# Moving the quantisation of the second FFN weight out of the attention stage, and broadcasting a row of scales by DMA

## The chip, the cores and the metric

The kernel runs on the 8 cores of one Trainium2 chip. Each core works on its own two sequences of 2048 tokens (16 sequences in all), and no data goes between cores. The metric is the device time of the slowest core, in microseconds, as the median over runs. The profile is one execution on its slowest core, core 6.

## The reference, cut to what matters

```python
# attention half, per sequence (S=2048, D=1024)
q, k, v = split(x @ w_qkv.T)
att = softmax(q @ k.T / 32)
y = einsum('bqk,bvd->bqd', att, v) @ w_fc.T + b_fc   # k and v are summed apart
x = LN(x + (LN(x + y) * gamma + beta))
# FFN half (H=4096): bit_linear, depthwise conv of 3 taps over tokens, SiLU, bit_linear
act_quant(t)    = clip(round(t * s), -128, 127) / s,  s = 127 / max|t| over the row
weight_quant(w) = clip(round(w * s), -1, 1) / s,      s = 1 / mean|w|
h = silu(conv(act_quant(x) @ weight_quant(w1).T))
x = LN(x + act_quant(h) @ weight_quant(w2).T)
```

In the einsum the rows of the attention matrix are summed by themselves, so the attention half needs each softmax row only as its own sum; the scores are computed all the same.

## The kernel before, in words

The program is a series of blocks. In a block each engine has its own list of instructions, executed in order; between blocks all engines meet. `p.wait(engine, sem, n)` puts a wait for a semaphore into an engine's list, and everything behind it on that engine waits too. SP (sync), ACT (scalar) and POOL (gpsimd) also issue DMAs, in the order of their lists.

1. **P0, W0.** Constants are loaded; w1T and w2T are streamed through SBUF to get the mean absolute values, in two buffers: the load of chunk c is issued when the buffer of chunk c-2 has been read (L214 to L231). `wqcols` then holds the scales of both weights.
2. **For each of two sequences:** `APRO` (q and k from x, the column sums of v), then `A3`. `A3` goes over 16 tiles of 128 queries: 32 matmuls of scores into four PSUM banks (L646), maxima on DVE (L655), exponentials with sums on ACT (L664), the epilogue of the *previous* tile (layer norms and the int8 quantisation of x, L297 to L399), then the row sums (L677 to L684). At the start of the first `A3`, POOL is given the 16 loads of x and wqT that the next sequence needs (L487, L417).
3. **In each of these 32 query tiles** one chunk of w2 (128 x 1024) is quantised by `emit_w2q_chunk`: POOL loads it into `q2st` two chunks ahead (L448, L477), ACT scales it into `q2z` (L456), DVE makes the ternary values in `t2st` (L464, L467), POOL stores them to the DRAM tensor `t2q` (L472).
4. **W1** (`quantize_weights(w1T, ...)`): DVE quantises w1 straight into the SBUF tensor `tw`, three instructions per chunk (L743, L746, L749), loads in two buffers.
5. **F1**, over 16 tiles of 256 tokens: 32 groups of 8 matmuls (L937), evicted by DVE with a scale (L948), conv by ACT (L961) and DVE (L825, L832), SiLU on ACT (L840). At the end of the tile DVE takes the maximum over all 4096 hidden values of each token (L977), and from it the scale of each token is worked out. The scales stand as a row in `rowbuf` (L1015); a matmul with `esel` spreads the row to 128 partitions (L1019), DVE copies it from PSUM (L1023) and doubles it three times (L1028), so that `s2bc8` holds 8 copies of the row in each partition. The hidden values are then quantised in four groups (`emit_quant_A`: L852 and L863; `emit_quant_B`: L875 to L888), inside the loop of the *next* tile; the first group's L852 stands ahead of the next tile's first eviction in DVE's list. After the loop of a tile SP issues the store of the quantised tile before it (L898) and eight transposing loads and one small load for the tile after next (L811, L815).
6. **F2**: SP loads `t2q` back into `tw` in 32 pieces (L1067), waits for them, loads three tiles of hidden values (`load_hq`, L1084) and TensorE multiplies (L1113, L1122); the FFN epilogue follows tile by tile.

Of the kernel before, what the change touches and what calls it, by code (L numbers as in the profile page):

```python
# [81 lines left out]
def build_program(cfg: Cfg, debug=False):  # L82
# [35 lines left out]
    t2q = nc.dram_tensor("t2q", [HC * 128, D], BF16, kind=ik).ap()  # L118
# [26 lines left out]
    zcol = sb("zcol", (128, 1), F32)  # L145
# [58 lines left out]
    p.op("vector", lambda v: v.memset(zcol[:], 0.0))  # L204
# [231 lines left out]
    q2st = attn_stack.enter_context(nc.sbuf_tensor("q2st", [128, 2 * D], F32))  # L436
    q2z = attn_stack.enter_context(nc.sbuf_tensor("q2z", [128, D], F32))
    t2st = attn_stack.enter_context(nc.sbuf_tensor("t2st", [128, D], BF16))
    w2_ld, w2_z, w2_st, w2_sz = {}, {}, {}, {}
    w2_next = [0]  # L440

    def emit_w2q_chunk(p, c):
        par = c % 2
        lsems = (dW, gX)
        ssems = (gg, gW)
        if c == 0:
            for cc in range(min(2, HC)):
                p.op("gpsimd", lambda g, cc=cc: g.dma_start(  # L448
                    out=q2st[:, (cc % 2) * D:(cc % 2 + 1) * D],
                    in_=w2T[cc * 128:(cc + 1) * 128, :]),  # L450
                    inc=lsems[cc % 2], k=16)
                w2_ld[cc] = lsems[cc % 2].n
        p.wait("scalar", lsems[par], w2_ld[c])
        if c >= 1:
            p.wait("scalar", vv, w2_z[c - 1])
        p.op("scalar", lambda sc, par=par: sc.activation(  # L456
            out=q2z[:], in_=q2st[:, par * D:(par + 1) * D],
            func=AF.Identity, scale=wqcols[:, 1:2], bias=zcol[:, 0:1]),
            inc=ssm)
        w2_sz[c] = ssm.n  # L460
        p.wait("vector", ssm, w2_sz[c])
        if c >= 1:
            p.wait("vector", ssems[(c - 1) % 2], w2_st[c - 1])
        p.op("vector", lambda v: v.tensor_scalar(  # L464
            out=t2st[:], in0=q2z[:], scalar1=0.5, scalar2=None,
            op0=ALU.is_ge))
        p.op("vector", lambda v: v.scalar_tensor_tensor(  # L467
            out=t2st[:], in0=q2z[:], scalar=-0.5, in1=t2st[:],
            op0=ALU.is_le, op1=ALU.subtract), inc=vv)
        w2_z[c] = vv.n  # L470
        p.wait("gpsimd", vv, w2_z[c])
        p.op("gpsimd", lambda g, c=c: g.dma_start(  # L472
            out=t2q[c * 128:(c + 1) * 128, :],
            in_=t2st[:]), inc=ssems[par], k=16)
        w2_st[c] = ssems[par].n
        if c + 2 < HC:
            p.op("gpsimd", lambda g, cc=c + 2: g.dma_start(  # L477
                out=q2st[:, (cc % 2) * D:(cc % 2 + 1) * D],
                in_=w2T[cc * 128:(cc + 1) * 128, :]),
                inc=lsems[par], k=16)  # L480
            w2_ld[c + 2] = lsems[par].n
    import math
    W2K = max(1, math.ceil(HC / (NSEQ * NGRP * NQT)))
# [9 lines left out]
    for s_i in range(NSEQ):  # L493
# [129 lines left out]
        if True:  # L623
            if True:
# [72 lines left out]
                if s_i == NSEQ - 1:
                    while w2_next[0] < HC:
                        emit_w2q_chunk(p, w2_next[0])
                        w2_next[0] += 1  # L700
# [60 lines left out]
    with nc.sbuf_tensor("xqF", [128, 2 * DC * WW], BF16) as xqF, \  # L761
# [18 lines left out]
        p.wait("sync", dW, dW.n)  # L780
        p.wait("sync", gX, gX.n)
        p.wait("sync", gg, gg.n)
        p.wait("sync", gW, gW.n)
# [124 lines left out]
        for i in range(NT1):  # L908
# [340 lines left out]
```

How the kernel before makes its waits and increments, by code:

```python
        def cl(e, fn=fn, tgt=tgt, drain=drain):  # L52
            ins = fn(e)
            if tgt is not None:
                ins.then_inc(*tgt)
            if drain:
                e.drain()
# [3 lines left out]
    def wait(self, eng, sem, val):  # L61
        self.items[eng].append(lambda e, h=sem.h, v=val: e.wait_ge(h, v))
```

## Time and profile before

| | before |
|---|---|
| median of 3 runs | 4906.04 us (4904.6 to 4906.8) |
| time of the profiled execution | 4904.37 us |
| its span on core 6, from first to last instruction | 4902.7 us |
| spans of the eight cores | 4890.1 to 4902.7 us |
| mean granted TensorE clock | 0.701 to 0.704 of full speed |
| busy: DVE, PE, ACT, POOL | 66%, 37%, 21%, 1% |
| share of the chain that ended last: DVE, PE, issue, ACT | 38%, 12%, 4%, 3% |

The busy share says how long an engine had an instruction in work. The chain is the work that ended last, followed back through what released each step. A line such as `[0.51 <-ACT q2z L456]` in a timeline says that the engine had idled 0.51 us before this instruction and that ACT's instruction of line 456 ended that. In what follows, stages are read with timelines, since an average over the span mixes stages with different limits.

### The profile page before, as it was taken

How to read it: one execution, taken by the hardware profiler on the slowest of the kernel's cores; microseconds unless marked ns; L12 is line 12 of the kernel's file. 1: busy time of each engine (PE TensorE's matmuls, PEld its weight loads, DVE VectorE, ACT ScalarE, POOL GpSimd, SP SyncE). 2: the span in 40 equal slices, each digit the busy share in tenths (PEclk: the TensorE clock that was granted, in tenths of full speed). 3: DMA queues.
4: the chain of work that ended last, by engine and by line, in shares of the span. 5: the costliest groups of instructions: out<-in, count | busy, mean ns of one | idle time of the engine just before them, and what ended most of it. 6: DMA issues, size and time to landing. Idle time of an engine off the chain costs nothing.

```text
span 4902.7 us, 35148 instructions; the slowest of 8 cores (4890.1 to 4902.7 us)
## 1 busy us (share of the span) xinstructions
PE 1817.2 (37%) x8417; PEld 920.3 (19%) x8500; DVE 3256.1 (66%) x4491; ACT 1007.3 (21%) x1805; POOL 60.2 (1%) x116
## 2 busy tenths in 40 slices
PE   0046232217532311323333323333333332307999
PEld 0022011103111101211221112111121221203444
DVE  3313087872278777788888888888888888872333
ACT  2200022210022221222222222222222222210111
POOL 0000000000000000000000000000000000000000
PEclk9998666658766655665656666666566666658999
DMA  5521422221222214000000000000000000016543
GB/s 167 151 39 35 99 73 71 69 67 18 69 67 69 71 54 147 7 23 23 3 21 24 23 23 2 22 23 24 23 3 21 23 23 18 4 35 197 167 142 108
DMA packets 196433, 275.74 MB, mean 56 GB/s; under 512 B 64514, under 2 KB 132354, under 8 KB 194180
## 3 DMA queue, kind: packets, MB, share of 16 engines
q1 hardware_dynamic: 163716, 189.57, 13.2%
q0 software_dynamic: 14080, 41.95, 3.7%
q10 hardware_dynamic: 18432, 41.97, 2.2%
q14 instruction: 135, 1.11, 0.1%
q8 instruction: 70, 1.15, 0.1%
HBM read 196.86 MB, written 83.91 MB: 57 GB/s over the span
## 4 chain that ended last, share of the span: by engine, by line
DVE 38%; PE 12%; issue 4%; ACT 3%; DVEq 2%; DMA 1%; SPq 1%; ACTq 0%
DVE accb L885 6%; DVE maxM L977 5%; DVE vt L832 4%; DVE vt L825 4%; DVE rbuf L882 4%; DVE ubuf L948 3%; DVE hqst L888 3%; DVE dsb L875 3%; PE ps_d L1122 2%; DVE zscr L852 2%; PE ps_s L1122 2%; PE ps_c L1113 2%; PE ps_s L1113 2%; DVEq L57 2%; ACT vt L961 1%
## 5 line engine op out<-in xcount | busy, mean ns | idle before, releaser
L937 PE MATMUL ps_a<-xqF,tw 128*128 128x258 bf16 (+1 forms) x1024 | 216.2, 382 | 1002.4 <-DVE ubuf L948 775.7
L646 PE MATMUL ps_s<-kf,qf 128*128 128x512 bf16 x1002 | 289.2, 455 | 641.9 <-ACT disc L664 636.8
L961 ACT ACTIVATE vt<-ubuf,cbcol,cwcol 128x256 f32<-128x256 f32 x512 | 307.7, 601 | 921.7 <-DVE ubuf L948 891.9
L937 PE MATMUL ps_s<-xqF,tw 128*128 128x258 bf16 (+1 forms) x2048 | 316.7, 309 | 52.2 <-DVE ubuf L948 49.5
L885 DVE TENSOR_TENSOR accb<-accb,rbuf 128x2048 bf16<-128x2048 bf16 x256 | 313.4, 1224 | 19.7 <-issue 0.9
L937 PEld LDWEIGHTS ps_a<-xqF,tw 128*128 128x128 bf16 x1024 | 123.5, 128 | 1078.9 <-issue 1038.0
L825 DVE SCALAR_TENSOR_TENSOR vt<-ubuf,cwcol,vt 128x256 f32<-128x256 f32 x512 | 248.1, 485 | 84.1 <-issue 57.2
L832 DVE SCALAR_TENSOR_TENSOR vt<-ubuf,cwcol,vt 128x256 f32<-128x256 f32 x512 | 248.1, 485 | 39.2 <-issue 1.1
L840 ACT ACTIVATE ubuf<-vt 128x256 f32<-128x256 f32 x512 | 213.7, 417 | 269.3 <-DVE vt L832 251.8
L646 PEld LDWEIGHTS ps_s<-kf,qf 128*128 128x128 bf16 x1024 | 113.1, 113 | 818.7 <-issue 743.5
L984 PE MATMUL ps_c<-identf,maxM 128*128 128x128 f32 x64 | 19.1, 454 | 643.6 <-DVE maxM L977 643.6
L977 DVE TENSOR_REDUCE maxM<-ubuf 128x256 f32<-128x8192 f32 x16 | 247.5, 15466 | 10.2 <-ACT ubuf L840 10.2
L863 ACT ACTIVATE iqq<-zscr,c 128x2048 int32<-128x2048 f32 x64 | 128.1, 2002 | 603.6 <-DVE zscr L852 603.6
L1122 PE MATMUL ps_d<-tw,hq 128*128 128x512 bf16 x512 | 195.6, 382 | 126.1 <-DMA hq<-hqs 125.1
L937 PEld LDWEIGHTS ps_s<-xqF,tw 128*128 128x128 bf16 x2048 | 210.5, 109 | 163.8 <-issue 116.0
L937 PE MATMUL ps_b<-xqF,tw 128*128 128x258 bf16 (+1 forms) x1024 | 217.5, 384 | 12.4 <-DVE ubuf L948 10.8
L507 PE MATMUL ps_a<-xfb,wbuf 128*128 128x512 bf16 x501 | 126.3, 394 | 225.1 <-DMA wbuf<-wqT 82.0
L1122 PE MATMUL ps_s<-tw,hq 128*128 128x512 bf16 x512 | 194.0, 379 | 1.1
L882 DVE TENSOR_SCALAR rbuf<-dsb 128x2048 bf16<-128x2048 bf16 x256 | 177.6, 694 | 20.0 <-issue 0.4
L1113 PE MATMUL ps_c<-tw,hq 128*128 128x512 bf16 x492 | 188.0, 382 | 0.0
L1113 PE MATMUL ps_s<-tw,hq 128*128 128x512 bf16 x491 | 186.1, 379 | 0.0
L875 DVE SCALAR_TENSOR_TENSOR dsb<-zscr,iqq 128x2048 bf16<-128x2048 f32 x64 | 146.7, 2292 | 21.4 <-issue 10.8
(144 smaller groups left out, 3026.8 us busy)
## 6 DMA issues: line engine op xcount, KB each, us to landing
hqs<-hqst SPq DMA_DIRECT2D x16, 2048.0 KB, 8.9
wstage<-w1T SPq DMA_DIRECT2D x8, 2048.0 KB, 8.7
wstage<-w2T SPq DMA_DIRECT2D x32, 512.0 KB, 4.4
xres<-x_tm SPq DMA_DIRECT2D x32, 512.0 KB, 4.7
q2st<-w2T POOLq DMA_DIRECT2D x32, 512.0 KB, 3.8
x1s<-x1t ACTq DMA_DIRECT2D x32, 512.0 KB, 5.2
qstage<-w1T SPq DMA_DIRECT2D x8, 2048.0 KB, 8.4
xres<-x1s SPq DMA_DIRECT2D x32, 512.0 KB, 7.4
```

The costliest lines, as they stand in the source:

```text
L646: t.matmul(ps_s[kb][:, 0:KBW], qf[:, dc * S + qcol: dc * S + qcol + 128], kf[:, dc * S + kb * KBW: dc * S + (kb + 1) * KBW], start=(dc == ...
L825: v.scalar_tensor_tensor(out=vt2[:, cpar * T1W2:cpar * T1W2 + T1], in0=ubuf[:, hc * T1W2:hc * T1W2 + T1], scalar=cwcol[:, 3 * hc:3 * hc + ...
L832: v.scalar_tensor_tensor(out=vt1[:, cq * T1W2:cq * T1W2 + T1], in0=ubuf[:, hc * T1W2 + 2:hc * T1W2 + 2 + T1], scalar=cwcol[:, 3 * hc + 2:3 ...
L840: p.op("scalar", lambda sc, hc=hc, cq=cq: sc.activation(out=ubuf[:, hc * T1W2 + 1:hc * T1W2 + 1 + T1], in_=vt1[:, cq * T1W2:cq * T1W2 + T1 ...
L875: p.op("vector", lambda v, FD=FD: v.scalar_tensor_tensor(out=dsb[:, 0:FD], in0=zscr[:, 0:FD], scalar=128.0, in1=iqq[:, 0:FD], op0=ALU.add, ...
L882: p.op("vector", lambda v, FD=FD, thr=thr: v.tensor_scalar(out=rbuf[:, 0:FD], in0=dsb[:, 0:FD], scalar1=thr, scalar2=None, op0=ALU.is_ge))
L885: p.op("vector", lambda v, FD=FD: v.tensor_tensor(out=accb[:, 0:FD], in0=accb[:, 0:FD], in1=rbuf[:, 0:FD], op=ALU.add))
L937: lo=lo, hi=hi, w0=w0, W=W: t.matmul(bank[:, 0:W], tw[:, dc * H + hc * 128: dc * H + hc * 128 + 128], xqF[:, (par * DC + dc) * WW + (lo - w0):
L961: p.op("scalar", lambda sc, hc=hc: sc.activation(out=vt1[:, (hc % 4) * T1W2:(hc % 4) * T1W2 + T1], in_=ubuf[:, hc * T1W2 + 1:hc * T1W2 + 1 ...
L977: p.op("vector", lambda v: v.reduce_max(out=maxM[:, 0:T1], in_=_ap(ubuf, 1, [[HC * T1W2, 128], [1, T1], [T1W2, HC]]), axis=AX.X, apply_abs ...
L1113: banks=banks: t.matmul(banks[0][:, 0:DH], hq2[:, slot + hc * T1 + sq * 128: slot + hc * T1 + sq * 128 + 128], tw[:, hc * D + 0:hc * D + D ...
L1122: banks=banks: t.matmul(banks[1][:, 0:DH], hq2[:, slot + hc * T1 + sq * 128: slot + hc * T1 + sq * 128 + 128], tw[:, hc * D + DH:hc * D + ...
```

## The change

Three edits.

- **w2 is no longer quantised in the attention stage.** `emit_w2q_chunk`, its three buffers, its semaphores, the DRAM tensor `t2q` and the reload of it at the start of F2 go. In their place `quantize_weights(w2T, HC, D, 1)` stands as a block between F1 and F2 and writes `tw` directly: 32 chunks of 128 x 1024, each with one load and three DVE instructions, in two buffers.
- **The row of scales is spread by DMA.** The matmul with `esel`, the PSUM copy and the three doubling copies go. SP stores `rowbuf` (256 fp32) to a DRAM tensor `s2row`, waits for that store, and loads `s2bc8` from it with a source that repeats the row for 128 partitions and 8 copies: 1 MB in runs of 1 KB.
- **DVE waits for that load** ahead of the first `emit_quant_A` of a tile, and no longer right behind the row's computation.

```diff
-    t2q = nc.dram_tensor("t2q", [HC * 128, D], BF16, kind=ik).ap()
+    s2row = nc.dram_tensor("s2row", [2, T1], F32, kind="Internal").ap()
...
-    def emit_w2q_chunk(p, c):
...
-                    for _ in range(W2K):
-                        if w2_next[0] < HC:
-                            emit_w2q_chunk(p, w2_next[0])
-                            w2_next[0] += 1
...
+            if g0 == 0:
+                p.wait("vector", s2sems[i % 2], s2_ld[i])
             p.op("vector", lambda v, g0=g0, ng=ng, FD=FD, s28=s28: v.tensor_tensor(
...
             p.wait("vector", mm, mm.n)
+            if i >= 1:
+                p.wait("vector", s2sems[(i - 1) % 2], s2_ld[i - 1])
             p.op("vector", lambda v: v.tensor_copy(
                 out=rowbuf[0:1, 0:T1], in_=ps_d[0:1, 0:T1]), inc=vv)
             ev_row = vv.n
-            p.wait("tensor", vv, ev_row)
-            p.op("tensor", lambda t: t.matmul(
-                ps_d[:, 0:T1], esel[:], rowbuf[:, 0:T1], start=True, stop=True),
-                inc=mm)
-            p.wait("vector", mm, mm.n)
-            p.op("vector", lambda v: v.tensor_copy(
-                out=s2bc8[:, 0:T1], in_=ps_d[:, 0:T1]), inc=vv)
-            w = T1
-            while w < NQG * T1:
-                cw2 = min(w, NQG * T1 - w)
-                p.op("vector", lambda v, w=w, cw2=cw2: v.tensor_copy(
-                    out=s2bc8[:, w:w + cw2], in_=s2bc8[:, 0:cw2]))
-                w += cw2
-            p.op("vector", lambda v: v.engine_nop(), inc=vv)
+            sem = s2sems[i % 2]
+            if i >= 2:
+                p.wait("sync", sem, s2_ld[i - 2])
+            p.wait("sync", vv, ev_row)
+            p.op("sync", lambda s, i=i: s.dma_start(
+                out=s2row[i % 2:i % 2 + 1, 0:T1], in_=rowbuf[0:1, 0:T1]),
+                inc=sem, k=16)
+            p.wait("sync", sem, sem.n)
+            if i >= 1:
+                p.wait("sync", vv, lastA_ev[i - 1])
+            p.op("sync", lambda s, i=i: s.dma_start(
+                out=_ap(s2bc8, 0, [[NQG * T1, 128], [T1, NQG], [1, T1]]),
+                in_=_ap(s2row.tensor, (i % 2) * T1,
+                        [[0, 128], [0, NQG], [1, T1]])), inc=sem, k=16)
+            s2_ld[i] = sem.n
...
+    quantize_weights(w2T, HC, D, 1)
...
-        for c in range(HC):
-            sem = dS if c % 2 == 0 else dSb
-            p.op("sync", lambda s, c=c: s.dma_start(
-                out=tw[:, c * D:(c + 1) * D],
-                in_=t2q[c * 128:(c + 1) * 128, :]), inc=sem, k=16)
-        t2_dS, t2_dSb = dS.n, dSb.n
-        p.wait("tensor", dS, t2_dS)
-        p.wait("tensor", dSb, t2_dSb)
```

## Rows read from the trace of the kernel before

**Rows 1.** Page, part 1: busy time and share of each engine.

```profile
PE 1817.2 (37%) x8417; PEld 920.3 (19%) x8500; DVE 3256.1 (66%) x4491; ACT 1007.3 (21%) x1805; POOL 60.2 (1%) x116
```

**Rows 2.** Windows, F1: stretch, its length, busy of each engine, PEclk, DMA share, GB/s.

```profile
1936.00:4399.00 2463.00, 781.55 (x4256) 491.01 (x4256) 2027.53 (x2752) 650.82 (x1089) 0.00 (x0) 0.63 0.07 18
```

**Rows 3.** Timeline, first two query tiles: start, length, engine, line, out<-in, idle before.

```profile
540.84 9.00 PE L646 MATMUL ps_s<-kf,qf 128*128 128x512 bf16 x31 [8.18 <-ACT disc L664]
541.57 0.75 DVE L684 TENSOR_SCALAR atile<-wrowbc,colsb 128x1024 f32<-128x1024 f32 x1
...
606.95 0.53 POOL L448 DMA_DIRECT2D q2st<-w2T  x1 [3.48 <-issue]
...
614.22 2.99 DVE L655 TENSOR_REDUCE colsb<-ps_s 128x1 f32<-128x512 f32 x4 [0.17 <-issue]
```

**Rows 4.** Timeline, a query tile in the steady state.

```profile
700.28 0.75 DVE L684 TENSOR_SCALAR atile<-wrowbc,colsb 128x1024 f32<-128x1024 f32 x1
...
703.70 2.99 DVE L655 TENSOR_REDUCE colsb<-ps_s 128x1 f32<-128x512 f32 x4 [0.16 <-issue]
...
710.48 9.52 PE L646 MATMUL ps_s<-kf,qf 128*128 128x512 bf16 x32 [20.75 <-ACT disc L664]
...
733.85 2.99 DVE L655 TENSOR_REDUCE colsb<-ps_s 128x1 f32<-128x512 f32 x4 [0.17 <-issue]
```

**Rows 5.** Timeline, second query tile of the second sequence.

```profile
1358.51 2.99 DVE L655 TENSOR_REDUCE colsb<-ps_s 128x1 f32<-128x512 f32 x4 [5.81 <-PE ps_s L646]
```

**Rows 6.** Timeline, the boundary between the second and the third tile of F1.

```profile
2161.76 0.58 SPq L815 DMA_DIRECT2D f1bc<-f1s  x1
...
2178.26 0.41 DVE L1015 COPY rowbuf<-ps_d 1x256 f32<-1x256 f32 x1 [1.26 <-PE ps_d L1010]
...
2183.33 2.29 DVE L852 TENSOR_TENSOR zscr<-ubuf,s2bc 128x2048 f32<-128x2048 f32 x1
2185.77 2.00 ACT L863 ACTIVATE iqq<-zscr,c 128x2048 int32<-128x2048 f32 x1 [28.92 <-DVE zscr L852]
...
2189.47 0.48 DVE L825 SCALAR_TENSOR_TENSOR vt<-ubuf,cwcol,vt 128x256 f32<-128x256 f32 x1 [0.16 <-ACT vt L961]
```

**Rows 7.** Timeline, SP: a 4 KB row stored to DRAM, and the load that waits for it.

```profile
486.28 0.30 SPq L565 DMA_DIRECT2D vrow_d<-vrow  x1
487.56 3.67 SPq L569 DMA_DIRECT2D colsb<-vrow_d  x8
```

**Rows 8.** DMA issues: out<-in, issuer, count, KB each, median us from issue to landing.

```profile
hqs<-hqst SPq DMA_DIRECT2D x16, 2048.0 KB, 8.9
...
wf<-wfcT SPq DMA_DIRECT2D x16, 512.0 KB, 4.0
...
f1bc<-f1s SPq DMA_DIRECT2D x12, 129.0 KB, 3.2
```

**Rows 9.** Windows, while three 4 KB rows are broadcast to 128 partitions: the columns as in rows 2.

```profile
5.00:12.00 7.00, 0.00 (x0) 0.00 (x0) 0.00 (x0) 0.00 (x0) 0.00 (x0) 1.00 0.84 215
```

**Rows 10.** Timeline, from the end of F1 to the first matmul of F2.

```profile
4396.72 2.29 DVE L888 TENSOR_TENSOR hqst<-accb,iqq 128x2048 bf16<-128x2048 bf16 x1
...
4408.45 19.40 SPq L1067 DMA_DIRECT2D tw<-t2q  x32
4437.06 13.81 SPq L1084 DMA_DIRECT2D hq<-hqs  x3
4447.44 0.10 PEld L1113 LDWEIGHTS ps_c<-tw,hq 128*128 128x128 bf16 x1 [125.43 <-issue]
```

**Rows 11.** Timeline, W0 on w2T: two of its steps on ACT, nine apart.

```profile
123.87 1.06 ACT L227 ACTIVATE wabs<-wstage 128x1024 f32<-128x1024 f32 x1 [1.50 <-DMA wstage<-w2T]
...
149.19 1.06 ACT L227 ACTIVATE wabs<-wstage 128x1024 f32<-128x1024 f32 x1 [1.93 <-DMA wstage<-w2T]
```

**Rows 12.** Groups of instructions by form: count, busy us, mean ns, idle before.

```profile
L467 DVE SCALAR_TENSOR_TENSOR t2st<-q2z,t2st 128x1024 bf16<-128x1024 f32 x32 | 39.2, 1224 | 2.4
...
L464 DVE TENSOR_SCALAR t2st<-q2z 128x1024 bf16<-128x1024 f32 x32 | 22.2, 693 | 87.0 <-ACT q2z L456 86.7 <-issue 0.2
```

More of the change, by code:

```diff
@@ L144, in build_program @@
     c128 = sb("c128", (128, 1), F32)
-    zcol = sb("zcol", (128, 1), F32)
     gammaBC = sb("gammaBC", (128, D), F32)
@@ L175, in build_program @@
     gg = Sem(E(nc.semaphore("gg")))
-    dW = Sem(E(nc.semaphore("dW")))
-    gW = Sem(E(nc.semaphore("gW")))
-    gX = Sem(E(nc.semaphore("gX")))
     p = PB(nc, "P0")
@@ L203, in build_program @@
     p.op("vector", lambda v: v.memset(rowbuf[:], 0.0))
-    p.op("vector", lambda v: v.memset(zcol[:], 0.0))
     p.op("vector", lambda v: v.memset(wsmat[:], 0.0))
@@ L435, in build_program @@
     dGq = {}
[L436 to L440, printed above, removed]
-    def emit_w2q_chunk(p, c):
[L443 to L483, printed above, removed]
     def emit_A0(p, s_i):
@@ L692, in build_program @@
                     epi_q[qt] = (row0, par, sto, dep, ldsem)
-                    for _ in range(W2K):
-                        if w2_next[0] < HC:
-                            emit_w2q_chunk(p, w2_next[0])
-                            w2_next[0] += 1
[L697 to L700, printed above, removed]
                 qt_last = NGRP * NQT - 1
@@ L779, in build_program @@
         p.wait("sync", dS, dS.n)
[L780 to L783, printed above, removed]
         def tgeom(i):
@@ L801, in build_program @@
         ld_cnt = {}
+        s2_ld = {}
+        lastA_ev = {}
+        s2sems = (dS, dSb)
         def emit_loads(i):
@@ L857, in emit_quant_A @@
             ev_z = vv.n
+            lastA_ev[i] = ev_z
             p.wait("scalar", vv, ev_z)
@@ L1059, in build_program @@
         p.wait("sync", dXb, dXb.n)
-        p.wait("sync", dG, dG.n)
-        p.wait("sync", dW, dW.n)
-        p.wait("sync", gX, gX.n)
-        p.wait("sync", gg, gg.n)
-        p.wait("sync", gW, gW.n)
-        for c in range(HC):
-            sem = dS if c % 2 == 0 else dSb
-            p.op("sync", lambda s, c=c: s.dma_start(
-                out=tw[:, c * D:(c + 1) * D],
-                in_=t2q[c * 128:(c + 1) * 128, :]), inc=sem, k=16)
-        t2_dS, t2_dSb = dS.n, dSb.n
-        p.wait("tensor", dS, t2_dS)
-        p.wait("tensor", dSb, t2_dSb)
         hq_ld = {}
@@ L1149, in build_program @@
     p.wait("gpsimd", dG, dG.n)
-    p.wait("gpsimd", dW, dW.n)
-    p.wait("gpsimd", gX, gX.n)
-    p.wait("gpsimd", gg, gg.n)
-    p.wait("gpsimd", gW, gW.n)
     p.run()
```

## The prediction, made before the changed kernel ran

> **What bounds the kernel now.** I read the page first: DVE is busy for two thirds of the span, TensorE for little more than a third [rows 1]. Then I cut the span into stages. In F1, half of the whole time, DVE is busy 2027.5 of 2463 us and ACT and PE far less [rows 2]: DVE's list sets the pace, and what stands between its instructions at a tile's boundary is paid 16 times. The timelines of the attention stage say the same with two exceptions. In the steady state DVE begins the maxima L655 of the next tile with no wait for TensorE, and the 9.52 us of matmuls end at 720.0, far ahead of their use at 733.85 [rows 4]. The exceptions are the first chunk of each sequence: in the first, DVE has finished L684 at 542.32 and begins L655 at 614.22, because the first w2 load is behind POOL's 16 loads for the next sequence and issued at 606.95 [rows 3]; in the second, L655 waits for TensorE anyway [rows 5]. At the end of F1 everything waits for DMAs for 48.4 us, from L888's end at 4399.01 to the first matmul's weights at 4447.44 [rows 10]. All three edits touch such places, so I price them by timeline.
>
> **Part 1: w2 leaves the attention stage (a gain).** In the steady state the stretch from L684's end (701.03) to L655 (703.70) is 2.67 us: a wait for ACT, 0.69 and 1.22 us of work [rows 4, 12]. Without the chunk, a semaphore wait of 0.16 us is left, so 2.51 us are saved. This holds for 30 chunks: all but the first of each sequence. 30 x 2.51 = 75.3 us. Chunk 16, the first of the second sequence, saves nothing, for L655 waits for TensorE [rows 5]. Chunk 0 saves its stall: its matmuls end at 540.84 + 9.00 = 549.84 [rows 3], so L655 can begin at 549.95 in place of 614.22, a gain of 64.3 us. Together -139.6 us. What is next late there? Not TensorE: the period falls from 30.15 (733.85 - 703.70) to 27.6 us, and the matmuls end some 16.3 us after L655 begins (710.48 + 9.52 - 703.70) [rows 4]. POOL's 16 loads now run beside a busy DVE; all were issued by 606.95, some 80 us into the stage [rows 3], and the second sequence needs them only when 16 tiles of 27.6 us, 442 us, are over, so even at three times the length they are hidden; without that cover each further us would count fully.
>
> The page "SBUF — State Buffer" of the Trainium skill states in its note on the "DVE blocks DMA" trap that descriptors made by GpSimd wait while DVE runs certain fp32 instructions. By it these loads would be slower in the new kernel; no stretch of rows here shows 16 of them beside a busy DVE, and by the bound above it would change the sum only past some 440 us of loading.
>
> **Part 2: the row of scales goes by DMA (a loss).** Now: L1015 ends at 2178.67, L852 begins at 2183.33, 4.66 us later [rows 6]. After: SP issues the store about 0.08 us behind L1015, is free to do so (its last issue for the tile ended at 2162.3 [rows 6]), and can issue the load 1.28 us later, as for the 4 KB row in [rows 7]. The load of 1 MB takes D, then DVE wakes in 0.1. So L852 begins 1.46 + D behind L1015. The memset and the scaling of the next tile's factors are done in this time, so TensorE starts the next tile earlier, and the four evictions behind L852 no longer wait for it: L825 came 6.14 us after L852's start [rows 6]; ACT needs L852's 2.29, 0.15, its own 2.00, 0.14 and 0.60 of the first conv instruction, 5.3 with the wait, so 0.84 us come back in 15 of 16 tiles. Queued behind DVE's wait are these evictions, and ACT and TensorE wait with them; on SP nothing is queued that is due for over 100 us. Sum: 16 x (1.46 + D - 4.66) - 15 x 0.84 = 16 D - 63.8.
>
> D has no row. Loads of 512 KB land in 4.0 us, 2 MB in 8.9 us also in runs of 512 bytes [rows 8]; on the line between them 1 MB takes 5.6, of which 2.4 are fixed. But the source is one 1 KB row read 1024 times. Broadcasts of 4 KB rows moved at 215 GB/s on average with other small transfers between them [rows 9]: 1.05 MB / 215 = 4.9 us, with the fixed 2.4 that is 7.3, and somewhat less without those others. Broadcasting one 1 KB row to 128 partitions takes 3.2 us for 129 KB [rows 8]; with the 1.28 of [rows 7] as its fixed part, eight times the rest is 15.4, so 16.6 in all is the upper bound. The lower bound is the 4.0 of half the bytes. I take 6.0, between the first two and nearer to the size rows, since the 215 GB/s were shared: 16 x 6.0 - 63.8 = +32 us. The bounds give 0 and +202.
>
> The page "DMA: Bandwidth & Descriptors" of the Trainium skill (Anatomy of one DMA) states 2.0 us for any DMA and 436 GB/s on top, for the other way of issuing. By it the store and the load together are an estimated 6.4 us where I take 7.3, and the sum of this part would be an estimated +18.
>
> **Part 3: w2 between F1 and F2 (a loss).** Three instructions per chunk: 0.75 (L684 has this shape), 0.69 and 1.22 us [rows 4, 12], 2.83 with gaps, 3.0 with a wait. Load c is issued when chunk c-2 is finished. So two chunks take one load and one computation, if the load is the longer. W0 has the same scheme on the same tensor: nine steps in 25.32 us, 2.81 each, and 2 x 2.81 - 1.06 = 4.56 us from release to use [rows 11]. The 4.0 us load of the same size [rows 8] gives 4.1. W1 asks for less per us, so I take 4.2: (4.2 + 2.83) / 2 = 3.5 us per chunk; the bounds are 3.0 (DVE alone) and 3.7. The first load is behind the 2 MB store of the last tile: issued right behind L888's end at 4399.0, landed 8.9 later [rows 8, 10], then 512 KB more (1.6 us by the line of part 2), so the first chunk begins at about 4410. 4410 + 31 x 3.5 + 2.8 = 4521.3 is its end. A change of block costs 0.5 (the store lands at 4408.0, L1067 follows at 4408.45), and from `load_hq`'s issue to the first matmul it is 4447.44 - 4437.06 = 10.4 [rows 10]. TensorE starts at 4532.2 in place of 4447.4: +85 us; with the bounds +69 and +91. Nothing hides it, since F2 needs all of `tw` and all engines meet between blocks. The reload's 32 issues and their wait are in the 48.4 us that are replaced. F2 itself is unchanged.
>
> **The sum.** -139.6 + 32 + 85 = -23 us. The profiled execution took 4904.4, so 4882; the median of the runs is 1.7 above that execution: **4883 us**.
>
> **The rivals.**
>
> *The broadcast is slow.* 1024 reads of one 1 KB row of DRAM may not run at the rate of a spread load. For it speaks the 129 KB broadcast at 3.2 us, hardly faster than four times its size [rows 8]; against it, 215 GB/s with 4 KB rows [rows 9]. With D at the 8.9 of a 2 MB transfer the part costs +79 us and the kernel takes 4930; at the upper bound 5053. It decides for slower (by over 0.2%) from D = 8.0 on, where 16 D - 63.8 - 54.6 = 9.8. Chance 0.18.
>
> *The edits cancel.* D between 6.8 and 8.0 puts the sum within 0.2% (9.8 us, about what a measurement can tell from no change); 7.4 gives 4905. For it: the 7.3 of the broadcast row. Chance 0.14.
>
> *The losses are smaller.* D near 4.5, and chunks at DVE's 3.0 us, since fewer bytes per us are asked than in W0: -139.6 + 8 + 69 = -62, so 4843. Chance 0.08.
>
> *The stall only moves.* If the first tile's epilogue then waits for its residual load, or the second sequence for POOL's loads, part 1's 64 us are lost: 4947. Against it: POOL's loads have 360 us of cover, and SP issues the residual loads with nothing ahead of them. Chance 0.03.
>
> The likeliest case has what is left, 0.57. **Numbers.** Faster 0.57 + 0.08 = 0.65, same 0.14, slower 0.21. The range runs from 4846 (the smaller losses nearly in full) to 4936 (D at 8.9 with chunks at 3.7), leaving out the slowest broadcasts and the moved stall; the likeliest case alone reaches from 4862 to 4895.
>
> **What would show it.** L655 of the second query tile begins at about 550 and the period is 27.6 us. At each boundary of F1, L852 begins 7.5 us after L1015's end, released by the DMA into `s2bc8`, and L825 5.3 after L852. W1's second use shows DVE idle some 0.7 us before each L743, ended by a DMA, and 111 us in all. I am wrong if the broadcast's landing is far from 6.0, where each us is worth 16; if the chunks are off 3.5, each 0.1 worth 3; or if something in F1 that this trace does not show changes its pace.

## The result: slower, by the broadcast alone

| | before | after |
|---|---|---|
| median (10 runs of each) | 4907.42 us (4902.93 to 4970.47) | 5137.61 us (5086.43 to 5229.99) |
| ratio | | 1.0438 [1.0391, 1.0484] |
| time of the profiled execution | 4904.37 us | 5086.43 us |
| its span on the slowest core | 4902.7 us (core 6) | 5084.9 us (core 4) |

The forecast was 4883 us with 4846 to 4936 as its range. The ratios leave out the runs in which one die's cores were granted a lower clock and took longer; the medians and ranges take in all. The runs of the changed kernel lie further apart than those of the kernel before, and its profiled execution, the one that everything below is worked out from, is the fastest of the ten, 51 us under the median; no trace shows where those 51 us lie. Since core 4 is its slowest core, I compare with core 4 of before, whose span was 4896.3 us: 188.6 us are to be found.

The page of after, part 1 (busy time of each engine), and of part 5 the group of the quantisation's first step (count, busy us, mean ns, then the idle time ahead of it):

```profile
PE 1827.8 (36%) x8468; PEld 925.7 (18%) x8468; DVE 3251.0 (64%) x4458; ACT 967.7 (19%) x1773; POOL 25.7 (1%) x52
...
L792 DVE TENSOR_TENSOR zscr<-ubuf,s2bc 128x2048 f32<-128x2048 f32 x64 | 146.7, 2292 | 336.0 <-DMA s2bc<-s2row 331.2
```

DVE has as much to do as before [rows 1]. What is new is idle time: 331.2 us ahead of the 16 first L792 (L852 of before), 20.7 us each, and a DMA ends it. I then cut the span at the marks at which the prediction cut it. First the attention stage, which ends where F1's first load is issued (the list of one tile's instructions: count, min/median/max ns, first and last start), after:

```profile
L749 SPq DMA_TRANSPOSE xqF<-xqs x128: 1111/1245/6854, 1776.3 to 4060.9; - x128
```

The same of before, core 4:

```profile
L811 SPq DMA_TRANSPOSE xqF<-xqs x128: 1113/1244/6837, 1917.8 to 3990.3; - x128
```

F1 begins 141.5 us earlier. Timeline of after's first query tiles on core 4, which answers to [rows 3, 4]:

```profile
532.43 8.82 PE L593 MATMUL ps_s<-kf,qf 128*128 128x512 bf16 x32 [8.19 <-ACT disc L611]
533.16 0.75 DVE L631 TENSOR_SCALAR atile<-wrowbc,colsb 128x1024 f32<-128x1024 f32 x1
...
541.36 2.99 DVE L602 TENSOR_REDUCE colsb<-ps_s 128x1 f32<-128x512 f32 x4 [7.45 <-PE ps_s L593]
...
568.13 0.75 DVE L631 TENSOR_SCALAR atile<-wrowbc,colsb 128x1024 f32<-128x1024 f32 x1
569.04 2.99 DVE L602 TENSOR_REDUCE colsb<-ps_s 128x1 f32<-128x512 f32 x4 [0.16 <-issue]
...
579.58 0.53 POOL L412 DMA_DIRECT2D wbuf<-wqT  x1 [18.22 <-issue]
...
596.72 2.99 DVE L602 TENSOR_REDUCE colsb<-ps_s 128x1 f32<-128x512 f32 x4 [0.52 <-issue]
```

The second tile's maxima L602 no longer wait for a w2 chunk: they follow their matmuls, which end at 541.25. From L631's end (568.88) to L602 (569.04) are the forecast 0.16 us, and the period is 27.68 us (596.72 - 569.04). On core 6, the core of [rows 3], the second tile's L602 begins at 549.81, where "about 550" was forecast.

Now a boundary in F1, the first, to hold against [rows 6]:

```profile
1880.27 0.41 DVE L958 COPY rowbuf<-ps_d 1x256 f32<-1x256 f32 x1 [1.26 <-PE ps_d L951]
1880.76 0.24 SPq L965 DMA_DIRECT2D s2row<-rowbuf  x1
...
1881.94 0.40 SPq L971 DMA_DIRECT2D s2bc<-s2row  x1
...
1905.35 2.29 DVE L792 TENSOR_TENSOR zscr<-ubuf,s2bc 128x2048 f32<-128x2048 f32 x1 [23.72 <-DMA s2bc<-s2row]
1907.74 2.00 ACT L804 ACTIVATE iqq<-zscr,c 128x2048 int32<-128x2048 f32 x1 [48.88 <-DVE zscr L792]
1910.58 0.48 DVE L763 SCALAR_TENSOR_TENSOR vt<-ubuf,cwcol,vt 128x256 f32<-128x256 f32 x1 [0.59 <-ACT vt L902]
```

And the last one:

```profile
4412.97 0.36 SPq L971 DMA_DIRECT2D s2bc<-s2row  x1
4429.78 2.29 DVE L792 TENSOR_TENSOR zscr<-ubuf,s2bc 128x2048 f32<-128x2048 f32 x1 [18.12 <-DMA s2bc<-s2row]
```

From the load's issue to its use, which I call D from here on (the profile gives no landing for this transfer), are 23.4 us at the first boundary and 16.8 at the last. Over the 16 boundaries of core 4 the sum is 324.6 us, 20.3 each; the means of the eight cores go from 17.7 to 20.3. From the first load to the end of the last tile F1 took 4503.43 - 1776.3 = 2727.1 us, against 4394.79 - 1917.8 = 2477.0 on core 4 of before: +250.1.

Last, from the end of F1 to F2, for [rows 10]:

```profile
4501.14 2.29 DVE L829 TENSOR_TENSOR hqst<-accb,iqq 128x2048 bf16<-128x2048 bf16 x1
4503.55 0.36 SPq L839 DMA_DIRECT2D hqs<-hqst  x1
4504.43 107.23 SPq L678 DMA_DIRECT2D qstage<-w2T  x32
4515.18 0.75 DVE L682 TENSOR_SCALAR qz<-qstage,wqcols 128x1024 f32<-128x1024 f32 x1 [11.76 <-DMA qstage<-w2T]
...
4615.38 0.75 DVE L682 TENSOR_SCALAR qz<-qstage,wqcols 128x1024 f32<-128x1024 f32 x1 [0.89 <-DMA qstage<-w2T]
4619.00 13.77 SPq L1015 DMA_DIRECT2D hq<-hqs  x3
4629.40 0.58 PE L1044 MATMUL ps_c<-tw,hq 128*128 128x512 bf16 x1 [218.34 <-DMA hq<-hqs]
```

The same two ends on core 4 of before:

```profile
4392.50 2.29 DVE L888 TENSOR_TENSOR hqst<-accb,iqq 128x2048 bf16<-128x2048 bf16 x1
...
4442.29 0.10 PEld L1113 LDWEIGHTS ps_c<-tw,hq 128*128 128x128 bf16 x1 [124.51 <-issue]
```

L829's end at 4503.43 to L1044 at 4629.40 are 126.0 us; L888's end to L1113 were 47.5: +78.5. The three stretches give -141.5 + 250.1 + 78.5 = +187.1 of the 188.6 us. The 1.5 us left are F2's. Two of the three terms are close to the forecast ones; the surprise is the wait for `s2bc8`.

### The profile page after: what moved, and what is told of

Its sections match the earlier page's. It is cut to its first block and busy times, and to the rows that moved or that the text cites. A ratio compares the mean times of both kernels' runs of the same rounds, so it can differ in the third digit from the quotient of the medians.

```text
span 5084.9 us, 34871 instructions; the slowest of 8 cores (5027.7 to 5084.9 us)
## 1 busy us (share of the span) xinstructions
PE 1827.8 (36%) x8468; PEld 925.7 (18%) x8468; DVE 3251.0 (64%) x4458; ACT 967.7 (19%) x1773; POOL 25.7 (1%) x52
## 3 DMA queue, kind: packets, MB, share of 16 engines
q1 hardware_dynamic: 180388, 214.75, 16.6%
## 5 line engine op out<-in xcount | busy, mean ns | idle before, releaser
L878 PE MATMUL ps_a<-xqF,tw 128*128 128x258 bf16 (+1 forms) x1024 | 226.8, 396 | 1237.7 <-DVE ubuf L889 1033.6
L792 DVE TENSOR_TENSOR zscr<-ubuf,s2bc 128x2048 f32<-128x2048 f32 x64 | 146.7, 2292 | 336.0 <-DMA s2bc<-s2row 331.2
L878 PE MATMUL ps_s<-xqF,tw 128*128 128x258 bf16 (+1 forms) x2048 | 327.0, 317 | 45.0 <-DVE ubuf L889 42.1
L763 DVE SCALAR_TENSOR_TENSOR vt<-ubuf,cwcol,vt 128x256 f32<-128x256 f32 x512 | 248.2, 485 | 90.1 <-issue 54.1
L1044 PE MATMUL ps_c<-tw,hq 128*128 128x512 bf16 x512 | 195.8, 382 | 218.3 <-DMA hq<-hqs 218.3
L878 PE MATMUL ps_b<-xqF,tw 128*128 128x258 bf16 (+1 forms) x1024 | 230.5, 402 | 15.3 <-DVE ubuf L889 14.0
L1044 PE MATMUL ps_s<-tw,hq 128*128 128x512 bf16 x512 | 194.0, 379 | 0.0
L823 DVE TENSOR_SCALAR rbuf<-dsb 128x2048 bf16<-128x2048 bf16 x256 | 177.6, 694 | 20.7 <-issue 1.3
```

What stands on the lines that cost most here:

```text
L763: v.scalar_tensor_tensor(out=vt2[:, cpar * T1W2:cpar * T1W2 + T1], in0=ubuf[:, hc * T1W2:hc * T1W2 + T1], scalar=cwcol[:, 3 * hc:3 * hc + ...
L823: p.op("vector", lambda v, FD=FD, thr=thr: v.tensor_scalar(out=rbuf[:, 0:FD], in0=dsb[:, 0:FD], scalar1=thr, scalar2=None, op0=ALU.is_ge))
L878: lo=lo, hi=hi, w0=w0, W=W: t.matmul(bank[:, 0:W], tw[:, dc * H + hc * 128: dc * H + hc * 128 + 128], xqF[:, (par * DC + dc) * WW + (lo - w0):
L1044: banks=banks: t.matmul(banks[0][:, 0:DH], hq2[:, slot + hc * T1 + sq * 128: slot + hc * T1 + sq * 128 + 128], tw[:, hc * D + 0:hc * D + D ...
```

## The experiments

### One part alone: which of them costs

The first kernel is the changed one with the matmul and the doubling copies put back, so it has parts 1 and 3. The second is the kernel before with the DMA broadcast alone, part 2.

```diff
 # matmul back, against the changed kernel; DMA only is the reverse on the kernel before
-            if g0 == 0:
-                p.wait("vector", s2sems[i % 2], s2_ld[i])
...
-            p.op("sync", lambda s, i=i: s.dma_start(
-                out=_ap(s2bc8, 0, [[NQG * T1, 128], [T1, NQG], [1, T1]]),
-                in_=_ap(s2row.tensor, (i % 2) * T1,
-                        [[0, 128], [0, NQG], [1, T1]])), inc=sem, k=16)
+            p.op("tensor", lambda t: t.matmul(
+                ps_d[:, 0:T1], esel[:], rowbuf[:, 0:T1], start=True, stop=True),
+                inc=mm)
```

Matmul back:

> The changed kernel with the old spreading of the scales (matmul, PSUM copy, doubling copies) put back, so only the moves of w2 are left. Theory: the broadcast by DMA is the whole loss, the moves of w2 give what the trace of the changed kernel shows, -141 us in the attention stage and +78 us between F1 and F2, so 4907 - 63 = 4844 us, a clear gain. Rival: the moves of w2 cost something in F1 too (TensorE or DVE at another pace), then F1 is longer than the 2463 us of before and the time is 4907 or above.

DMA only:

> The kernel before with only the broadcast by DMA put in; w2 stays in the attention stage. Theory: the two parts add up, so this costs what is left of the change's 230 us once the 63 us of gain are taken out: 4907 + 293 = 5200 us, between 5150 and 5240, with about 20 us from the load's issue to its use. Rival: the broadcast is slow only because the cores reach it at other times or in another order in the changed kernel; then it is clearly faster here, below 5100.

Matmul back: 4855.28 us (median of 5 runs) beside 4915.58 of before on the same chip, ratio 0.9835 [0.9693, 0.9978]. DMA only: 5206.3 us (4 runs), ratio 1.0541 [1.0413, 1.0668], with a mean D of 21.3 us over all cores. Its page has the wait in the kernel that keeps the w2 work where it was:

```profile
L858 DVE TENSOR_TENSOR zscr<-ubuf,s2bc 128x2048 f32<-128x2048 f32 x64 | 146.7, 2292 | 389.7 <-DMA s2bc<-s2row 385.2
```

So parts 1 and 3 together are a gain of 60 us between the medians, where 54.6 were forecast; the ratio's interval leaves its size open between 0.2% and 3.1%. The stages say more: with the matmul back F1 took 2475.6 us in the mean of the cores, 2476.4 before, so the rival that the moved w2 work costs something in F1 is out. With the broadcast alone F1 took 2742.6 us. The broadcast is the whole loss, also without parts 1 and 3.

### What makes the broadcast slow

Candidates: the megabyte itself, its runs of 1 KB or SBUF's side of it; or the source, one row of 1 KB read 1024 times. The first kernel reads 1024 different runs of 1 KB from `w1T`, with everything else equal; what it loads are then not the scales, so it leaves the spreading of the scales out. The second stores the row eight times side by side and reads runs of 8 KB.

```diff
 # other source: the load reads w1T
-                in_=_ap(s2row.tensor, (i % 2) * T1,
-                        [[0, 128], [0, NQG], [1, T1]])), inc=sem, k=16)
+                in_=_ap(w1T.tensor, 0,
+                        [[H, 128], [2 * T1, NQG], [1, T1]])), inc=sem, k=16)
 # 8 KB row: the store
+                out=_ap(s2row.tensor, (i % 2) * 8 * T1,
+                        [[8 * T1, 1], [T1, 8], [1, T1]]),
+                in_=_ap(rowbuf, 0, [[512, 1], [0, 8], [1, T1]])),
 # 8 KB row: the load
+                out=_ap(s2bc8, 0, [[NQG * T1, 128], [1, NQG * T1]]),
+                in_=_ap(s2row.tensor, (i % 2) * 8 * T1,
+                        [[0, 128], [1, NQG * T1]])), inc=sem, k=16)
```

Other source:

> The changed kernel with one edit: the 1 MB load reads 1024 different 1 KB runs (of w1T) in place of one row 1024 times, so size, runs and target are the same; the row is still stored and waited for. The scales in s2bc8 are then not the right ones, so the output is not the reference's. Theory (a repeated source is slow): about 5.6 us from issue to use, 16 x 15 us less than the changed kernel, so 4860 to 4880 us. Rival (1 MB in 1024 runs of 1 KB into 8 KB per partition is slow from any source): 15 to 23 us as in the changed kernel, 5080 to 5150 us.

8 KB row:

> The changed kernel with the row stored 8 times side by side (8 KB) and read by each partition as one run of 8 KB. Same bytes moved, 128 reads in place of 1024, over a source eight times as long. Theory that the length of the source region sets the rate: about 5 to 8 us, near 4880 us. Theory that it is any rereading of few bytes by all cores, whatever the region: 15 us and more, above 5050 us.

The timeline of the other source at a boundary:

```profile
2059.69 0.57 SPq L971 DMA_DIRECT2D s2bc<-w1T  x1
...
2065.65 2.29 DVE L792 TENSOR_TENSOR zscr<-ubuf,s2bc 128x2048 f32<-128x2048 f32 x1 [6.32 <-DMA s2bc<-w1T]
```

The same of the 8 KB row:

```profile
2041.94 0.33 SPq L973 DMA_DIRECT2D s2bc<-s2row  x1
...
2046.78 2.29 DVE L792 TENSOR_TENSOR zscr<-ubuf,s2bc 128x2048 f32<-128x2048 f32 x1 [6.07 <-DMA s2bc<-s2row]
```

With the other source D is 5.96 us here and 6.1 in the mean of all cores, the 6.0 of the forecast, and the kernel took 4880.69 us (one run) where the forecast said 4883. So size, run length, destination, queue and the semaphores' way are cleared: the term was right for a source that is spread. (That the time comes so near has luck in it: F1 was 8 us and the w2 block 10 us shorter there than forecast, and its slowest core, 0, came to F1's first load at 1801.2, 25 us later than core 4 of the changed kernel.) The 8 KB row has a mean D of 4.95 us and took 4860.65 us in the profiled execution and 4960.46 in the other (before: 4915.58); of so scattered a pair only the stages of the profile can be used, and D says that a row may well be repeated, if it is long.

The rate can be read from windows of the load (columns as in [rows 2], the last is GB/s). After, during its first broadcast:

```profile
1894.00:1896.00 2.00, 0.00 (x0) 0.00 (x0) 0.00 (x0) 0.00 (x0) 0.00 (x0) 0.50 0.52 36
1896.00:1898.00 2.00, 0.00 (x0) 0.00 (x0) 0.00 (x0) 0.00 (x0) 0.00 (x0) 0.50 0.60 39
1898.00:1900.00 2.00, 0.00 (x0) 0.00 (x0) 0.00 (x0) 0.00 (x0) 0.00 (x0) 0.50 0.83 79
...
1902.00:1904.00 2.00, 0.00 (x0) 0.00 (x0) 0.00 (x0) 0.00 (x0) 0.00 (x0) 0.50 1.00 87
```

The other source:

```profile
1910.00:1911.00 1.00, 1.00 (x6) 0.73 (x5) 0.00 (x0) 0.00 (x0) 0.00 (x0) 0.50 1.05 348
```

The 8 KB row:

```profile
1892.00:1893.00 1.00, 1.00 (x6) 0.69 (x5) 0.00 (x0) 0.00 (x0) 0.00 (x0) 0.50 0.98 410
```

The DMA engines are up to fully busy in each, but move 36 to 87 GB/s from the one row in these windows, against 348 and 410. A busy share of 1.00 says that packets are in work, not that bytes flow.

### How much source is enough, and does its place matter

Four more kernels, whose lines differ only in store and load: a row of 2 KB (the row twice); eight copies 1280 bytes apart, read in runs of 1 KB; eight copies 64 KB apart; and one copy per partition (128 KB) that DVE doubles three times.

```diff
 # 2 KB row (the load writes its copies in runs of 2 KB too)
...
+                in_=_ap(s2row.tensor, (i % 2) * 2 * T1,
+                        [[0, 128], [0, NQG // 2], [1, 2 * T1]])), inc=sem, k=16)
 # eight rows, 1280 bytes apart
+                in_=_ap(s2row.tensor, (i % 2) * 2560,
+                        [[0, 128], [320, NQG], [1, T1]])), inc=sem, k=16)
 # eight rows, 64 KB apart
+                in_=_ap(s2row.tensor, (i % 2) * 131072,
+                        [[0, 128], [16384, NQG], [1, T1]])), inc=sem, k=16)
 # 128 KB load
+                out=_ap(s2bc8, 0, [[NQG * T1, 128], [1, T1]]),
+                in_=_ap(s2row.tensor, (i % 2) * T1,
+                        [[0, 128], [1, T1]])), inc=sem, k=16)
```

2 KB row:

> The changed kernel with the row stored twice side by side (2 KB) and read by each partition in four runs of 2 KB: the dose between one row of 1 KB (about 20 us) and one of 8 KB (5.0 us). If the rate grows with the source's length, 1 MB takes half as long as from 1 KB, 2 us fixed plus 9: about 11 us. If there is a step somewhere above 2 KB, it stays near 20.

Eight rows, 1280 bytes apart:

> The changed kernel with the row stored 8 times at a distance of 1280 bytes, and the 8 copies of each partition read each from its own row. Still 1024 reads of 1 KB, still few bytes in all, but each row is read 128 times and the rows span 10 KB. Theory (what is short is the rate at which one 1 KB row of DRAM can be read by all 16 DMA engines and all cores at once): as with the 8 KB row, 5 to 7 us from issue to use. Rival (the 8 KB runs made the load fast, not the longer source): 15 us and more.

Eight rows, 64 KB apart:

> The same with the 8 rows 64 KB apart. Theory of the row as the unit: again 5 to 7 us. If the distance matters in the other direction (rows at a large power of two fall on the same part of DRAM), then as slow as one row, 15 us and more.

128 KB load:

> The changed kernel with a load of only one copy per partition (128 reads of the 1 KB row, 128 KB) and the seven other copies made by DVE as before (256, 512 and 1024 columns, 1.8 us). Theory: the slow rate hits an eighth of the bytes, so about 3.2 to 4.5 us of load and with the doubling 5 to 6.5 us from the load's issue to the quantisation; 4860 to 4885 us. If the first read of the row were what is slow, it would stay above 10 us.

Each is one run, with one run of 4909.91 us of the kernel before beside it. D is the mean over all cores and boundaries; the changed kernel and the two kernels above stand in the table too. In the kernel before, F1 took 2476.4 us.

| source of the load | D, us | least and most, us | F1, us (mean of the cores) | kernel, us |
|---|---|---|---|---|
| one row of 1 KB, 1 MB (after) | 18.8 | 14.3 to 23.6 | 2702.9 | 5086.43 (profiled) |
| eight rows 64 KB apart, 1 MB | 17.8 | 13.0 to 21.6 | 2701.7 | 5082.63 |
| one row of 2 KB, 1 MB | 9.6 | 8.0 to 16.3 | 2564.7 | 4954.16 |
| eight rows 1280 bytes apart, 1 MB | 6.2 | 5.5 to 9.1 | 2515.0 | 4918.86 |
| 1024 runs of `w1T`, 1 MB | 6.1 | 5.8 to 7.1 | 2500.1 | 4880.69 |
| one row of 8 KB, 1 MB | 5.0 | 4.3 to 7.8 | 2494.8 | 4860.65 (profiled) |
| one row of 1 KB, 128 KB | 3.1 | 2.9 to 4.4 | 2477.0 | 4835.66 |

The eight rows 64 KB apart, timeline:

```profile
2061.38 0.37 SPq L973 DMA_DIRECT2D s2bc<-s2row  x1
2082.59 2.29 DVE L792 TENSOR_TENSOR zscr<-ubuf,s2bc 128x2048 f32<-128x2048 f32 x1 [22.43 <-DMA s2bc<-s2row]
```

The eight rows 1280 bytes apart, page, part 5:

```profile
L792 DVE TENSOR_TENSOR zscr<-ubuf,s2bc 128x2048 f32<-128x2048 f32 x64 | 146.7, 2292 | 132.1 <-DMA s2bc<-s2row 127.2
```

The 128 KB load, timeline:

```profile
2035.13 0.33 SPq L974 DMA_DIRECT2D s2bc<-s2row  x1
...
2038.09 1.56 DVE L793 COPY s2bc<-s2bc 128x256 f32<-128x256 f32 x3 [3.30 <-DMA s2bc<-s2row]
2039.72 2.29 DVE L795 TENSOR_TENSOR zscr<-ubuf,s2bc 128x2048 f32<-128x2048 f32 x1
```

The 2 KB row, windows on core 0 during its first load:

```profile
1878.00:1880.00 2.00, 2.00 (x12) 1.36 (x10) 0.00 (x0) 0.00 (x0) 0.00 (x0) 0.50 0.59 175
1880.00:1882.00 2.00, 2.00 (x11) 1.41 (x10) 0.00 (x0) 0.00 (x0) 0.00 (x0) 0.50 0.71 143
```

Twice the row halves D, and its best window, 175 GB/s, is twice the 87 of the 1 KB row: here the rate went with the length of the row. Eight rows close together, still read in runs of 1 KB, are as good as a spread source. Eight rows 64 KB apart are as bad as one. So it is not the number of different rows that counts, but where in DRAM they lie: whatever serves the repeated reads is shared by addresses 64 KB apart and not by those 1280 bytes apart.

What that is, these runs don't say, nor whether it is the distance of 64 KB or its being a power of two that counts: no rows at a padded distance of that size were run. The theory of the row as the unit, expected for these rows, failed.

Of the 128 KB load 2.96 us go by from issue to use at this boundary: at 80 GB/s 1.6 of them are an estimate for the bytes. With this load and DVE's copies F1 is as long as with the matmul, and the kernel took 24 us less than the least expected.

F1's times follow from D and one more thing. The stores of eight copies hold the load back: it is issued 2.09 us behind such a store and 1.25 behind a store of one copy (means over all cores), which is 13 us in 16 tiles. So the 8 KB row should be 16 x (4.95 - 6.10) + 13 = 5 us faster in F1 than the other source, and is 5.3; the rows 1280 bytes apart 15 us slower, and are 14.9.

The kernel times follow less well. The one with rows 1280 bytes apart took 4918.86 us, the other source 4880.69, and 15 of these 38 us are F1's. Its core 6, with the longest span (4917.3), waits 7.95 us at a boundary (127.2 / 16), core 0 7.4, with a span of 4862.3. Core 6 came into F1 16 us later than core 0 (first load at 1784.8 and 1768.5), took 8 us longer over it and 31 over what follows, where its granted clock was 0.93 in F2 and that of core 0 1.00. So 47 of the 55 us between the two cores lie outside the stage in question, and I take nothing from that kernel's time.

### The gain without the loss

Four kernels test parts 1 and 3 by other means. The first is the kernel before with POOL's 16 loads dealt out over the query tiles, one each, so that the first w2 chunk is not behind them. The second takes, on top, the doubling copies out, and L852 reads its second operand with a step of 0 over the eight groups; so the copies' 1.4 us per boundary go with no DMA in their place. The third is the changed kernel with the matmul and the same step of 0. The fourth is the third with ACT doing the first of the three steps per w2 chunk, and the first three `hq` loads issued in that block.

```diff
 # loads dealt out (kernel before)
-                if s_i + 1 < NSEQ:
-                    emit_A0(p, s_i + 1)
...
+                    if s_i + 1 < NSEQ:
+                        emit_A0_part(p, s_i + 1, qt)
 # step of 0
-            s28 = s2bc8[:, 0:FD]
+            s28 = _ap(s2bc8, 0, [[NQG * T1, 128], [0, ng], [1, T1]])
...
-            w = T1
-            while w < NQG * T1:
...
 # ACT in the w2 block
+            p.op("scalar", lambda sc, stage=stage, z=z: sc.activation(
+                out=z[:], in_=stage[:], func=AF.Identity,
+                scale=wqcols[:, 1:2], bias=zcol[:, 0:1]), inc=ssm)
```

Loads dealt out:

> The kernel before with one edit: POOL's 16 loads for the second sequence are issued one per query tile, behind that tile's w2 chunk, in place of all 16 at the start. Theory: the stall of the first chunk (72 us, of which 64 count) came from its load standing behind these 16 on POOL, so it goes and nothing else changes: 64 us less, 4843 us where before is at 4907. Rival: the stall is only moved to a later chunk or to the start of the second sequence: within 10 us of before.

Loads dealt out, step of 0:

> The same, and the three doubling copies of the scales are left out: L852 reads its second operand 8 times over from one copy of 256 columns. Theory: the instruction takes its 2.29 us as before, and at each of 16 boundaries 1.9 us of copies go, some of which TensorE's first groups need; 20 to 30 us less than the spread alone, 4813 to 4823. Rival: reading an operand again with a step of zero is slower on DVE, then 64 instructions grow and the time is above the spread alone.

Changed kernel, matmul, step of 0:

> The changed kernel with the scales spread by the matmul and read with the step of zero. Theory: the moves of w2 are worth the same as the spread of POOL's loads (-141 + 78 against -64), so within 10 us of the kernel before this one, 4810 to 4825.

The same with ACT:

> As the last, and the w2 stage between F1 and F2 is made shorter: ACT scales a chunk and so frees its buffer for the next load, DVE has two instructions per chunk in place of three, and the first three loads of hidden values are issued at the end of this stage. A chunk took 3.2 us; with the buffer freed after ACT's 1.24 us two chunks take one load and one ACT instruction, about 2.5 us each, so 23 us less, and 5 to 10 us of the first load of F2 are hidden: 4780 to 4795. Rival: the loads of all cores at this rate take longer (W0 needed 2.8 us per chunk), then 4800 or more.

| | median, us (4 runs each) | least and most | ratio to before (4909.29) |
|---|---|---|---|
| loads dealt out | 4853.8 | 4842.19 to 4870.76 | 0.9885 [0.9841, 0.9928] |
| and step of 0 | 4815.72 | 4810.71 to 4912.66 | 0.9797 [0.974, 0.9853] |
| changed, matmul, step of 0 | 4818.24 | 4817.47 to 4853.84 | 0.9827 [0.9776, 0.9879] |
| the same with ACT | 4840.4 | 4795.68 to 4853.44 | 0.9839 [0.9773, 0.9904] |

Timeline of the loads dealt out, beginning of the stage:

```profile
527.56 0.53 POOL L448 DMA_DIRECT2D q2st<-w2T  x1 [146.32 <-POOLq L65]
...
546.87 0.69 DVE L464 TENSOR_SCALAR t2st<-q2z 128x1024 bf16<-128x1024 f32 x1 [0.16 <-ACT q2z L456]
```

The first w2 load is issued at 527.56 in place of 606.95 [rows 3], DVE quantises its chunk at 546.87, and the kernel gains 55.5 us between the medians; F1's first load comes at 1852.9 in the mean of the cores, against 1916.6 before, the expected 64 us. So of part 1's gain the 64 us of the stall need no move of the w2 work at all: they were the order of POOL's list. Groups of instructions of the kernel with the step of 0:

```profile
L863 DVE TENSOR_TENSOR zscr<-ubuf,s2bc 128x2048 f32<-128x2048 f32 x64 | 146.7, 2292 | 6.0 <-issue 0.2
```

L863 (L852 of before) still takes 2292 ns, and DVE waits 6.0 us in all ahead of it. The eight copies were never needed, neither by matmul nor by DMA. Taking them out is worth 38 us between the medians, but the two intervals overlap. The traces settle the size: F1 took 2445.4 to 2448.8 us on the eight cores with the step of 0, and 2474.8 to 2476.8 on those of the kernel with the loads dealt out alone, 29 us in the means. That is the copies' own 16 x 1.4 = 23 and what stood between them and their neighbours. The other 9 us of the medians are not F1's.

By its median this is the fastest kernel of the study, faster than the kernel before and the changed one. It and the third kernel (4818.24) came out as expected (4813 to 4823, 4810 to 4825). The third kernel's interval overlaps with it, so moving the w2 work is neither shown better nor worse than dealing out the loads.

The fourth missed its expected 4780 to 4795 and is not shown faster than the third: its lowest run is the lowest of all, its median is 22 us higher. Its own edit did work: from the end of F1 to the first matmul of F2 are 107.5 us in the mean of the cores, against 126.3 in the third, with a chunk every 2.6 to 2.8 us where it took 3.2. What hides these 19 us in its profiled execution lies ahead of F1, in what both kernels share: its slowest cores, 6 and 7, come to F1's first load at 1837 and 1832, its cores 0 to 3 at 1775 to 1791.

## Why the prediction was wrong, by its steps

**What bounds the kernel, right.** DVE's list set the pace of F1, and the boundary was paid 16 times; that is why 14.3 us more per transfer became 16 x 14.3 = 229.

**Part 1, right.** -141.5 us where -139.6 were forecast. Taken apart, in the medians over the cores: the first two L655 of the first sequence were 80.2 us apart and are 17.1, a gain of 63.1 (64.3 forecast), and a query tile with a chunk took 29.98 us and takes 27.44, a gain of 2.54 (2.51 forecast). That the whole agrees within 2 us is partly luck, since the cores of after come to F1's first load over a range of 20 us (1764.5 to 1784.7). POOL's loads do get slower beside the busy DVE: on core 4 their 16 issues go over 123.6 us, 75.9 before, with three gaps of 15.6 to 18.2 us and the others of 4.2 to 8.2. In kind this agrees with the page "SBUF — State Buffer" of the Trainium skill (the "DVE blocks DMA" trap), which the forecast had weighed. Nothing waits for them, so the forecast that this is hidden held.

**Part 2, the step that failed: "D has no row ... I take 6.0".** The form of the sum held: the store and the load are issued 1.18 us apart (1.28 forecast) and L763 comes 5.23 us behind L792 (5.3 forecast). With core 4's measured 324.6 us in place of 16 x 6.0 the sum gives 324.6 - 63.8 = +261, against +250.1 measured. D was mis-sized, 20.3 for 6.0, and that is 229 us; the kernel with a spread source shows that 6.0 was right for the bytes and runs that I had sized it by. The error is in the choice among rows: I weighed "nearer to the size rows" above the fact that the source was one row. The rival of the slow broadcast had this very mechanism; it had 0.18, with a price for 8.9 and one for the upper bound, and the range left the slowest broadcasts out.

A second, smaller size in this sum was wrong too, the other way. The 6.14 us from L852 to L825 were read at one boundary [rows 6]; over the 15 of core 4 of before they are 6.03 to 7.53, 6.80 in the mean, and 5.31 after. So 15 x 1.49 = 22 us come back and not 12.6, which is most of the 11 us between +261 and +250.1. The kernel with the spread source shows it again: its F1 is 23.7 us longer than before, where the sum with D at 6.1 gives 34.

**Its upper bound failed as well.** The 16.6 us were worked out from 129 KB in 3.2 us [rows 8], with 1.28 of them taken as fixed. That row did hold the rate of the windows' upper level: by an estimate from the 128 KB load, 128 KB at 80 GB/s are 1.6 us, which leaves 1.3 of the measured 2.96 as fixed, and with these 1 MB takes 13.1 + 1.3 = 14.4, near the least D of the changed kernel, 14.3. What it did not show is the level near 40 GB/s: the 16 small loads of a core stay short (DVE waits 56.2 to 57.8 us for them in all, 3.5 to 3.6 each, on every core), while the first of the large ones on core 4 spends over half its time there. The other witness, 215 GB/s for rows of 4 KB [rows 9], was a row four times as long; the runs now show that 2 KB already halve D and 8 KB end the effect. A bound has to come from a row with the same source and, where that one moved far fewer bytes, be left open above.

**Part 3, right.** +78.5 us where +85 were forecast, because a chunk took 3.23 us ((4615.38 - 4515.18) / 31) and not 3.5. The loads' 4.2 us from release to use, taken from W0, were too long by some 0.6; DVE's 2.83 us were right, and its idle time is what is left, 0.4.

**The rivals.** The moved stall did not come, and the edits did not cancel. "The losses are smaller" was right in part for the chunks (3.23 us, where it had 3.0) and wrong for D. Two figures of that part are a little off: D at 7.4 gives 4906 and not 4905, D at 8.0 gives 9.6 and not 9.8; the 4862 to 4895 of the likeliest case stand without their terms. The page "DMA: Bandwidth & Descriptors" of the Trainium skill gave with its anatomy an estimated +18 for part 2; it counts bytes and has no term for the source, so it would have missed by more than my own figure.

**What stays open.** After's windows show two levels, near 40 and near 80 GB/s, with nothing new on that core between them. On core 4 the lower one comes first; on core 0 it comes second:

```profile
1882.00:1884.00 2.00, 2.00 (x12) 1.44 (x11) 0.00 (x0) 0.00 (x0) 0.00 (x0) 0.58 0.42 88
...
1892.00:1894.00 2.00, 0.00 (x0) 0.00 (x0) 0.00 (x0) 0.00 (x0) 0.00 (x0) 0.50 0.39 36
```

D falls through F1; and cores 0 and 1, 2 and 3, 4 and 5, 6 and 7 have like sums (288.9 and 296.0, 291.3 and 283.5, 324.6 and 315.5, 308.2 and 298.7 us). It looks as if cores slowed each other and drifted apart later: two transfers that share a rate while they overlap would give such levels. No run with fewer cores at it was made, so this is argued and not shown, and so is whether the upper level, 87 GB/s, would hold for a core by itself. The same may be behind the changed kernel's spread from 5086 to 5230 us.

## What to carry to other kernels

Before you spread a small row by DMA, ask how long the stretch of DRAM is that the whole transfer reads: with 1 KB, on eight cores at about the same time, it ran at a tenth to a quarter of the rate that the same bytes made from a spread source, copies 64 KB apart did not help, and a small transfer hides it. If a wide operand only repeats, let the access pattern repeat it with a step of 0 and store it once. And when a stage begins with a stall, look at what its producer's queue was given first: putting 16 DMAs in another order was worth about as much as the whole move of the w2 work with its 78 us of new cost. And a gap that differs from tile to tile is to be read at all of its boundaries, not at one.

## What was unexpected of the hardware

- 1 MB loaded from one 1 KB row took 14.3 to 23.6 us from issue to use, at 36 to 87 GB/s in the windows shown; from a row of 2 KB 9.6 us, at up to 175 GB/s; from 1024 different runs of 1 KB 6.1 us, at 348 GB/s in one; from a row of 8 KB 5.0 us, at 410.
- Eight rows 64 KB apart took 17.8 us, eight rows 1280 bytes apart 6.2. The page "DMA: Bandwidth & Descriptors" of the Trainium skill (Latency and other measured facts) tells of copies whose rate falls when the rows of a DRAM tensor lie large powers of two apart: 207 GB/s at 512 KiB, 164 at 2 MiB, and 214 again at 4 MiB with 4 KiB of padding. The direction agrees with these two runs, but the case is another: here the same 1 KB rows are read over and over, 64 KB was far enough to be slow, and no padded distance of that size was run.
- The DMA engines' busy share was 1.00 at 87 GB/s and 0.98 at 410. In these windows the share says nothing of the rate.
- A DVE multiply of 128 x 2048 fp32 took 2292 ns with its second operand in memory in full, and 2292 ns with a step of 0 over eight groups.
